# Attention row totals from pre-added key blocks, a gate from a tanh, turned keys copied by ScalarE, a scan out of PSUM

## What is computed

```
Q = normalize(x @ W_q.T); K = normalize(x @ W_k.T); V = x @ W_v.T      # 16 heads, d_head 4, d_value 64
Qn = normalize(Q @ W_nudge)
scores = Qn @ K.T * 0.5 + k_bonus                                      # per key, from a product of gates
s = sigmoid(3 * (K @ simple_roots.T))                                  # the gates of k_bonus
attn = softmax(where(causal, scores, -inf)); out = attn @ V            # 256 x 256 for each head
x = x + layernorm(out @ W_out.T)
...                                                                    # FFN, recurrence, mixture of experts
```

## Time and profile before

| | before |
|---|---|
| median of three runs | 1771.08 us |
| the profiled execution: its own time | 1771.21 us |
| the profiled execution: its span | 1769.4 us |
| PE busy | 1639.8 us, 93% |
| DVE busy | 1318.6 us, 75% |
| ACT busy | 889.9 us, 50% |
| POOL busy | 1005.7 us, 57% |

### The profile page before, as it was taken

How to read it: one execution, slowest core, us unless ns; L and a number is a source line. 1 busy time by engine, 2 the same in 40 slices (tenths; PEclk the granted TensorE clock), 3 DMA queues, 4 the chain that set the end, 5 groups by cost and what they waited for, 6 DMA issues and landing times.

```text
span 1769.4 us, 47120 instructions
## 1 busy us (share of the span) xinstructions
PE 1639.8 (93%) x14871; PEld 1231.4 (70%) x14871; DVE 1318.6 (75%) x3869; ACT 889.9 (50%) x2003; POOL 1005.7 (57%) x1782
## 2 busy tenths in 40 slices
PE   3999999999999999859999999999999999689996
PEld 2677777777777777537778888878787886555553
DVE  5688888888888888645567777777777775758886
ACT  2666666666666666514444444444444443224443
POOL 5888888888888888722233333333333333327777
PEclk8999999999999999969999999999999999699998
DMA  1001111111111113010120000000000002534441
GB/s 42 11 29 55 54 54 54 54 54 54 54 54 54 54 54 104 14 36 13 50 81 22 31 28 29 27 30 29 26 30 28 26 25 75 178 123 133 133 132 41
DMA packets 78259, 95.96 MB, mean 54 GB/s; under 512 B 7046, under 2 KB 62995, under 8 KB 78160
## 3 DMA queue, kind: packets, MB, share of 16 engines
q1 hardware_dynamic: 70992, 77.91, 13.8%
q0 software_dynamic: 7168, 16.87, 2.7%
HBM read 53.14 MB, written 43.69 MB: 55 GB/s over the span
## 4 chain that ended last, share of the span: by engine, by line
PE 40%; DVE 7%; issue 4%; POOL 2%; DMA 1%; ACT 1%; DVEq 0%; POOLq 0%; SPq 0%; ACTq 0%
PE main L1329 6%; PE main L1331 5%; PE main L1338 5%; PE main L1487 4%; PE yp L1409 3%; PE xi L1244 2%; PE main L1269 2%; PE main L1282 2%; PE main L1393 2%; PE main L1396 1%; PE main L1394 1%; PE route L1501 1%; PE xi L1501 1%; PE turn L1237 1%; PE yp L1509 1%
## 5 line engine op out<-in xcount | busy, mean ns | idle before, releaser
L655 ACT ACTIVATE wgu<-score 128x384 f32<-128x384 f32 x512 | 223.2, 489 | 80.1 <-PE score L478 78.6
L1329 PE MATMUL main<-hT_high,h_high 128*128 128x512 f32 x512 | 221.2, 432 | 0.9 <-ACT hT_high L1586 0.9
L1331 PE MATMUL main<-hT_high,h_low 128*128 128x512 f32 x512 | 201.3, 393 | 0.0
L500 PE MATMUL outp<-wgu 128*32 128x256 f32 (+1 forms) x4096 | 194.5, 331 | 5.4 <-POOL wgu L323 4.3
L323 POOL TENSOR_SCALAR_AFFINE_SELECT wgu<-wgu 128x512 f32<-128x512 f32 x256 | 167.1, 658 | 46.1 <-ACT wgu L655 28.2
L500 PEld LDWEIGHTS outp<-wgu 128*32 128x32 f32 x4096 | 115.9, 110 | 70.6 <-issue 22.1
L1338 PE MATMUL main<-hT_low,h_high 128*128 128x512 f32 x512 | 138.3, 391 | 0.1
L1894 DVE SCALAR_TENSOR_TENSOR th<-th,main 128x512 f32<-128x512 f32 x64 | 43.9, 686 | 114.5 <-ACT th L1613 114.5
L536 PE MATMUL back<-wout,wgu 128*128 128x128 f32 x1024 | 128.6, 280 | 0.0
L536 PEld LDWEIGHTS back<-wout,wgu 128*128 128x128 f32 x1024 | 121.9, 195 | 0.4
L1227 POOL DMA_INDIRECT out<-res,idx x96 | 96.8, 1008 | 44.1 <-issue 40.5
(11 more groups left out here) (295 smaller groups left out, 4353.9 us busy)
## 6 DMA issues: line engine op xcount, KB each, us to landing
sorted_d<-row_buf SPq DMA_DIRECT2D x26, 772.0 KB, 3.7
xg<-sorted_d SPq DMA_DIRECT2D x48, 386.0 KB
wgu<-in_gate_up SPq DMA_DIRECT2D x4, 2048.0 KB
xa<-in_x SPq DMA_DIRECT2D x32, 128.0 KB, 3.5
xr<-in_x SPq DMA_DIRECT2D x32, 128.0 KB, 3.3
x_d<-x SPq DMA_DIRECT2D x32, 128.0 KB, 1.8
x1c<-x_d SPq DMA_DIRECT2D x16, 256.0 KB, 2.7
x1v<-x_d SPq DMA_DIRECT2D x16, 256.0 KB, 2.7
```

The costliest lines, as they stand in the source:

```text
L500: m = pe.matmul(outp[AUG * j:AUG * (j + 1), p % 2, k * P:T], val[par][:, k, h, v:v + AUG], weights(h, k), start=(k == 0), stop=(k == 1), t ...
L655: act.activation(prob[:, h // 2 % (RING // 2), :, h % 2, :], score[h % BANKS][:, 0:SC].rearrange("p (c q) -> p c q", q=P), ACT.Exp).then_i ...
L1329: pe.matmul(main[m % 2][:, :], w[0][:, k, m * P:(m + 1) * P], src[0][:, k, :], start=(k == 0), stop=False)
L1331: pe.matmul(main[m % 2][:, :], w[1][:, k, m * P:(m + 1) * P], src[0][:, k, :], start=False, stop=False)
```

## The change

There are four edits in the attention layer.

1. For queries 128 to 255 the row total is the sum over blocks 1 and 2. A new DVE instruction `fold` adds the two blocks of a group of four heads, 128 x 512 elements in float32, both operands in SBUF, into a new tile `folded` (two buffers). PE sums the folded tile instead of the two blocks. In a group PE now issues one set of 128-column sums for block 0 and one set of 128-column sums for the folded tile of the group before, where a set of 256 and a set of 128 columns stood. The exponentials of a head may overwrite the ring only when its group is folded. The reciprocal waits for the last folded sum.
2. The gate is 0.5 + 0.5 tanh(1.5 k): ACT takes a tanh in place of the exp, DVE one multiply-and-add in place of an add and a reciprocal.
3. ACT copies the turned keys out of PSUM, where DVE did.
4. The scan reads PSUM directly, with a constant tile `lowest` as its other operand, and the copy ahead of it is gone.

On DVE the scaling of xa (`xn`) also moves ahead of that of y (`yn`) and of the last residual.

```
             def fold(b, g):
+                wait(dve, s["masked"], PAIRS_A * b + 2 * g + 2)
+                wait(dve, s["p_fold"], GROUPS * b + g - 1)
+                first = 2 * g % (RING // 2)
+                dve.tensor_tensor(folded[:, g % 2].rearrange("p (r i) q -> p r (i q)", i=2),
+                                  prob[:, first:first + 2, 1].rearrange("p r i q -> p r (i q)"),
+                                  prob[:, first:first + 2, 2].rearrange("p r i q -> p r (i q)"),
+                                  ALU.add).then_inc(s["folded"], 1)
...
+            def folded_totals(b, g):
+                wait(pe, s["folded"], GROUPS * b + g + 1)
+                for j in range(GH):
+                    m = pe.matmul(total[AUG * j:AUG * (j + 1), P:T], pick[:, g, :], folded[:, g % 2, j, :],
+                                  start=False, stop=(g == GROUPS - 1), ...)
+                m.then_inc(s["p_fold"], 1)
...
-                for k in range(2):
-                    for j in range(GH):
-                        m = pe.matmul(total[AUG * j:AUG * (j + 1), k * P:T], pick[:, g, :], weights(GH * g + j, k), ...)
+                for j in range(GH):
+                    m = pe.matmul(total[AUG * j:AUG * (j + 1), 0:P], pick[:, g, :], prob[..., 0, h % 2, :], ...)
                 m.then_inc(s["p_sum"], 1)
+                if g > 0:
+                    folded_totals(b, g - 1)
+                if g == GROUPS - 1:
+                    folded_totals(b, g)
...
                     wait(act, s["p_sum"], GROUPS * b + (h - RING) // GH + 1)
+                    wait(act, s["folded"], GROUPS * b + (h - RING) // GH + 1)
...
-                    act.activation(ek[:], fr[:, :, 1], ACT.Exp, scale=-3.0).then_inc(s["ek"], 1)
+                    act.activation(ek[:], fr[:, :, 1], ACT.Tanh, scale=1.5).then_inc(s["ek"], 1)
...
+                    wait(act, s["p_kaT"], f + 1)
+                    act.activation(k_augT[1 - par][:].rearrange("p g t -> p (g t)"), turned_b[:, :], ACT.Copy)
...
-                    dve.tensor_tensor_scan(out=cmax[0:HEADS, :], data0=bonT[:], data1=bonT[:], initial=bonT[:, 0:1],
+                    dve.tensor_tensor_scan(out=cmax[0:HEADS, :], data0=lowest[:], data1=turned[0:HEADS, 0:T],
```

More of the change, by code:

```diff
@@ L157, in attention_layer @@
         k_augT = [sb(f"k_augT{i}", [P, GROUPS, T], BF16) for i in range(2)]
-        bonT = sb("bonT", [HEADS, T])
+        lowest = sb("lowest", [HEADS, T])
         cmax = sb("cmax", [P, T])
@@ L505, in weighted @@
                     wait(pe, s["rec"], b)
-                for k in range(2):
-                    for j in range(GH):
[L508 to L511, removed]
+                for j in range(GH):
+                    h = GH * g + j
+                    m = pe.matmul(total[AUG * j:AUG * (j + 1), 0:P], pick[:, g, :],
+                                  prob[:, h // 2 % (RING // 2), 0, h % 2, :], start=(g == 0), stop=(g == GROUPS - 1),
+                                  tile_position=(0, AUG * j), skip_group_check=True)
                 m.then_inc(s["p_sum"], 1)
+                if g > 0:
+                    folded_totals(b, g - 1)
+                if g == GROUPS - 1:
+                    folded_totals(b, g)
             def spread_out(z, g):
@@ L719, in step @@
                 if f is not None:
+                    wait(act, s["p_kaT"], f + 1)
+                    wait(act, s["p_score"], HEADS * (f - 1))
+                    act.activation(k_augT[1 - par][:].rearrange("p g t -> p (g t)"), turned_b[:, :],
+                                   ACT.Copy).then_inc(s["kaT"], 1)
                     wait(act, s["p_qaT"], f + 1)
@@ L785, in reciprocal @@
                     return
-                wait(dve, s["p_sum"], GROUPS * (z + 1))
+                wait(dve, s["p_fold"], GROUPS * (z + 1))
                 wait(dve, s["p_bc"], GROUPS * z)
@@ L834, in step @@
                 roots(n, f)
+                fold(b, 0)
                 normalise(z, par, 0)
@@ L865, in step @@
                                       -1.0, None, ALU.mult).then_inc(s["q5"], 1)
+                fold(b, 1)
                 normalise(z, par, 2)
@@ L896, in step @@
                 normalise(z, par, 3)
+                fold(b, 2)
+                if m is not None:
+                    wait(dve, s["rstd"], m + 1)
+                    wait(dve, s["p_xnT"], m)
+                    for i in range(TT):
+                        mm = dve.tensor_scalar(xn[:, i, :], xa[:, i, :], mv_ya[:, 1, i, 0:1],
+                                               rstd_ya[:, 1, i:i + 1], ALU.subtract, ALU.mult)
+                    mm.then_inc(s["xn"], 1)
+                fold(b, 3)
                 if y is not None:
@@ L906, in step @@
                     dve.tensor_tensor(x1[:], yn[:], xr[:], ALU.add).then_inc(s["x1"], 1)
-                if m is not None:
-                    wait(dve, s["rstd"], m + 1)
-                    wait(dve, s["p_xnT"], m)
-                    for i in range(TT):
-                        mm = dve.tensor_scalar(xn[:, i, :], xa[:, i, :], mv_ya[:, 1, i, 0:1],
-                                               rstd_ya[:, 1, i:i + 1], ALU.subtract, ALU.mult)
-                    mm.then_inc(s["xn"], 1)
             rounds(dve, step)
```

28 lines of the change are left out of this document (13 added, 15 removed).

## The result

Four runs of the changed kernel took 1852.58 to 1869.93 us, median **1857.62 us**; four runs of the kernel before beside them gave 1771.06. The ratio is 1.050, 95% interval 1.0473 to 1.0527: 86.6 us slower. The direction was forecast, the size was not (1789, range 1757 to 1808).

The account below looks back on a forecast made before the run. PE and POOL were taken as two bounds 0.43 us apart, with POOL becoming the bound: step 22.40 to 23.08 us, +20.4 us over 30 steps, less 2 at the start, from 1771.2 to 1789 us, range 1757 to 1808.

Parts of the forecast that it names:

- the ring of DVE: Rival: inverse root through DVE's chain back to POOL's split closes first, up to 0.5 us per step, 1804 us; chance 0.07.
- The folds' hold on POOL, 1.48 us: Four two-operand folds on DVE lengthen POOL's instructions by 0.29, 0.45, 0.45 and 0.29 us, together 1.48 us per step.
- The net on POOL, +1.11: POOL's added time per step: the folds' 1.48 us less 0.37 us given back by the scan's PSUM operand.
- its round of 23.08 us: POOL's own round per step, 21.97 + 1.11 us, above PE's 21.55, so it sets the step.
- POOL's gaps: Idle 0.15 to 0.16 us between a POOL instruction and the next that needs it, which no other engine's speed removes.
- PE's wait for masks: Sign to look for in the profile afterwards: this wait grown from 0.1 to over 1 us per step.
- PE's saving of 0.85 us: Per step, eight sets of 128-column sums on PE replace four of 256 and four of 128 columns.
- DVE's own 0.74 us: DVE gains 2.76 us of folds, loses 2.02 us; the 0.74 us per step fits its 2.3 us room, costing nothing.
- The scan: On DVE, reading one operand from PSUM, it no longer holds POOL up and gives back 0.37 us per step.
- The start, -2 us: While the pipeline fills, POOL waits 2.06 us for the gate; the shorter gate saves about 2 us, between 0 and 3.
- The exponentials of heads 8 and 9 behind the first fold: On ACT, waiting for that fold delays them 0.7 us; counted as 0 because it lies beside POOL's longer round.
- The rival on the other side: Folds cost POOL nothing and its old round is the floor: step 21.97 us, 1756 us; chance 0.15.

Follow-up runs that it names:

- e1: The changed kernel with only `yn` put back ahead of `xn` and the fourth fold on DVE; 1808.85 us, ratio 1.0234.
- e3: The changed kernel in its own order, with a second buffer for `y_sb` and nothing else changed; 1814.53 us, ratio 1.0262.
- e5: e4 plus four additions of 128x512 float32 at the folds' places, both operands in SBUF, result never read; 1802.94 us, ratio 1.0173.
- e6: e4 plus four one-operand tensor_reduce instructions, 512 to 256 elements, in place of the additions of e5; 1770.13 us, ratio 0.9998.
- e8: e1 with the first fold moved ahead of the Newton rounds and two buffers for `y_sb`; 1806.99 us.
- e9: The kernel before with the three small edits, only groups 1 and 2 folded, by tensor_reduce, DVE's old order at the step's end; 1764.40 us, ratio 0.9974.
- e4: The kernel before with the three small edits (tanh gate, keys copied by ACT, scan out of PSUM), no fold; 1770.03 us, ratio 1.0005.
- e7: e1 with the first fold moved ahead of the Newton rounds; 1808.63 us.
- e10: e8 with all four folds done by a one-operand tensor_reduce over blocks 1 and 2; 1780.40 us, ratio 1.0069.
- e13: The changed kernel in its own order, with `yn` late, its four folds done by a one-operand tensor_reduce; 1808.89 us, ratio 1.0235.

## Why the prediction was wrong

**The step that failed** is in the change part by part: what now stands ahead of `yn`, the moved `xn` and the fourth fold, had no term of its own. I followed the places of the folds against POOL and never asked what is queued behind `yn`. It was priced at nothing, with only "up to 0.5 us per step" for the ring of DVE in one rival of chance 0.07. That rival's ring ran through the Newton rounds back to POOL's split; the one that closed is another: root, `xn`, fold, `yn`, the single buffer `y_sb`, ACT's queue, the first mask. It costs 1.3 us per step at full clock (24.74 against 23.42), 2.2 on average in the profiled execution with its stretches at the lower clock (25.61), and 48.8 us in the medians, and two changes to it, the order (e1) and the buffer (e3), each take off 43 us or more. The waits before could have told it: DVE's wait of 24.8 us for the inverse root says that `yn` starts the moment the root is there, so that everything put in front of it delays it by its full length.

**The folds' hold on POOL, 1.48 us**: right. By the rows of e5 and e6 the four holds are 0.43, 0.42, 0.25 and 0.29 us, 1.39 together: two at the full price and two with a gap given back, as I had taken 0.45 and 0.29.

**The net on POOL, +1.11, and its round of 23.08 us**: too small by 0.17 and by 0.48. The small edits gave back 18.55 - 17.92 = 0.63 us, more than my 0.37. But the reduces of e6 already bring POOL from 17.92 to 18.24: the masks grow from 643 to 664 ns on average, two copies of query parts from 324 to 375, `bv` of L368 (L369 in e6) from 733 to 790. What makes them longer is not shown. The real folds of e8 bring it to 19.83, 0.22 above e5. The net is 19.83 - 18.55 = 1.28 us. POOL's gaps stayed as they were (22.42 - 0.43 - 18.55 = 3.44 before, 3.42 in e8; I had called them all 0.15 to 0.16 us, but two in each step, ahead of masks, are 0.31), and a wait of 0.31 us for exponentials was left where I had none. 0.17 and 0.31 are the 0.48 us from 23.08 to 23.56, some 14 of the 18 us by which e8 stands above the forecast. PE's wait for masks is 0.6 us per step in e8 (10.9 us in 17 steps) and not the 1 us and more that I had named as a sign.

**PE's saving of 0.85 us**: right. The two sums of the changed kernel:

```profile
L518 PE MATMUL total<-wgu,pick 128*32 128x128 f32 x504 | 27.4, 291 | 0.0
...
L488 PE MATMUL total<-folded,pick 128*32 128x128 f32 x508 | 22.7, 273 | 0.0
```

Instead of 576 instructions of 379 ns there are as many of 273 (partly at the lower clock). With POOL or the ring as the bound nothing of it arrives; in e9 it does.

**DVE's own 0.74 us cost nothing**: right. e6 adds 2.7 us to DVE per step and takes 1770.13.

**The scan** is back at its own length, and the copy behind it on POOL at 0.41:

```profile
L877 DVE TENSOR_TENSOR_SCAN cmax<-lowest,turned x16: 725/730/735, 200.7 to 585.3; 16x256 f32<-16x256 f32 x16
...
L425 POOL TENSOR_SCALAR k_aug<-k_part x16: 400/407/411, 202.9 to 587.6; 128x256 bf16<-128x256 bf16 x16
```

This is 0.96 and 0.78 in the earlier trace rows: as I had taken it, though no row had shown a scan with a PSUM operand.

**The start, -2 us**: wrong. With the shorter gate and no fold (e4) POOL starts the bonus 1.7 us earlier (21.54 against 23.27), but the first reciprocal only 0.2 us earlier (66.5 against 66.7): something else is last there. In the changed kernel it comes 2.0 us later.

**The exponentials of heads 8 and 9 behind the first fold, 0**: right. They wait 1.2 us in each step of e1 and not the 0.7 that I had taken, but e7 frees them and stays at e1's time.

**The chances.** The rival on the other side, folds that cost POOL nothing, is what e10 and e9 do with one operand, not what this change does.

**What stays open.** How much of the 49 us is clock can be bounded and not measured, since no run here holds the clock fixed. The steps at full clock are 1.3 us longer than e1's, an estimated 40 us in 30 steps, and the two runs at a mean clock of 0.970, that of e1, stand 44 to 46 us above it. The clock adds up to 17 us to the profiled execution and about 5 to the median. I have not found what the 0.31 us left of POOL's wait, the 0.32 us of busy time in e6 and the 6 to 8 us between e5 and e1 are made of.

## What to carry to other kernels

When an instruction is moved back in one queue, look for who waits for it, and then for what is queued behind the waiter: here one buffer of 256 elements per partition turned 2 us of lateness into 49 us on three other engines, and a second buffer, or the old order, undoes it. Before work is moved to VectorE beside a busy GpSimd, count its SBUF operands: four idle additions cost 33 us per launch and four tensor_reduce of like length nothing, the real folds cost 27 us less as tensor_reduce though each is longer, and an engine with room for the work is not enough. When two bounds stand 0.4 us apart, do only as much of an exchange as keeps the engine behind from becoming the bound: two folds without a hold gain, four, which fill VectorE, don't.

## What the runs showed of the hardware

- One addition of 128x512 with two SBUF operands lengthens the GpSimd instruction beside it by 0.25 to 0.43 us, inside that instruction's own duration, with no wait shown. A tensor_reduce of 0.68 us at the same place lengthens none of the three (e5 against e6).
- A tensor_reduce over two strided blocks, 1024 elements in and 512 out, takes 1.23 us, against 0.69 us for the two-operand addition alone and 0.93 us on average beside a busy GpSimd (e9, rows 6, e5).
- TensorE's granted clock fell to its lower level for some 7 us in every second step of the changed kernel's profiled execution, 56 of 400 us, where PE was 90% busy (88% in the steps at full clock), and not in e13, where it was 91% busy. Why the one and not the other, the traces do not show.
- A scan with one operand in SBUF and one in PSUM takes 0.73 us beside GpSimd, and the copy behind it 0.41, where a scan with two SBUF operands takes 0.96 and that copy 0.78.
